# Scatters that add scaled expert rows to the image's rows, two-expert tiles spread, and one run of tiles for all four units

## The reference, cut to what matters

```python
x = x + conv0(ln_c(x))                   # gate from two line convolutions, softmax over channels
t = t + moe0(ln_t(t))                    # 8 experts, top 2, shares renormalised, tanh gelu
x = x + conv1(ln_c(x))                   # max pools of 7 sizes, two of them weighted by a score
t = t + moe1(ln_t(t))                    # 8 experts, top 2, shares not renormalised, gelu
# moe: logits = x @ Wr + br; p = softmax(logits); two largest; y = sum share_e * (gelu(x W1_e + b1_e) W2_e + b2_e)
```

## Time and profile before

| what | us |
|---|---|
| median of 3 runs (lowest to highest) | 983.96 (982.83 to 988.96) |
| the profiled run's own time | 989.66 |
| its span, first to last instruction | 986.8 |

### The profile page before, as it was taken

The page is one execution under the profiler, slowest core; times in us unless marked ns, Lnnn a source line. Parts: engine busy times, 40 slices in busy tenths (PEclk is TensorE's granted clock), DMA queues, the critical chain, the costliest instruction groups (busy, mean ns, idle before and its releaser), DMA issues.

```text
span 986.8 us, 14530 instructions
## 1 busy us (share of the span) xinstructions
PE 758.5 (77%) x4233; PEld 656.6 (67%) x4233; DVE 555.5 (56%) x1262; ACT 520.6 (53%) x1407; POOL 608.4 (62%) x597
## 2 busy tenths in 40 slices
PE   0766249999988798975789499976689977988760
PEld 0535238988887586864788387865679866776760
DVE  7967953263500198999867198999985004100005
ACT  1602427475565465653177376653287754555644
POOL 1000057777777777888632777888754777777760
PEclk9886569999999989999589699998699999999985
DMA  9000255455578483544136773543147856656537
GB/s 356 5 0 1 85 204 160 133 176 162 198 238 286 120 308 128 175 149 129 43 106 227 236 257 123 179 150 126 41 119 237 287 193 220 202 160 239 181 101 255
DMA packets 56861, 165.23 MB, mean 167 GB/s; under 512 B 13888, under 2 KB 13901, under 8 KB 56528
## 3 DMA queue, kind: packets, MB, share of 16 engines
q1 hardware_dynamic: 38608, 128.87, 38.5%
q0 software_dynamic: 18176, 35.44, 12.0%
HBM read 134.89 MB, written 31.20 MB: 168 GB/s over the span
## 4 chain that ended last, share of the span: by engine, by line
DVE 32%; PE 31%; POOL 16%; issue 8%; DMA 6%; ACT 5%; SPq 1%; POOLq 0%; DVEq 0%; ACTq 0%
PE h_ps L787 9%; POOL xg L515 8%; PE yT_ps L800 8%; POOL y_rows L524 8%; DVE state L1290 6%; DVE work L1276 5%; DVE work L1271 5%; DVE tok L1240 4%; PE acc_ps L739 4%; DMA xg<-xn_rows,tile_rows 3%; PE turn_ps L722 3%; PE acc_ps L759 3%; DVE work L1284 2%; DMA work<-y_rows 2%; DVE work L986 2%
## 5 line engine op out<-in xcount | busy, mean ns | idle before, releaser
L515 POOL DMA_INDIRECT xg<-xn_rows,tile_rows x284 | 301.5, 1062 | 226.7 <-DVEq L1206 123.8
L524 POOL DMA_INDIRECT y_rows<-yr,tile_rows x284 | 302.4, 1065 | 127.7 <-issue 82.3
L787 PE MATMUL h_ps<-xT,expert 128*128 128x256 f32 (+1 forms) x1376 | 295.3, 365 | 6.8 <-ACT hT L600 5.5
L600 ACT ACTIVATE hT<-h_ps,expert 128x256 f32<-128x256 f32 (+1 forms) x688 | 250.3, 442 | 72.0 <-PE h_ps L787 71.7
L800 PE MATMUL yT_ps<-hT,expert 128*128 128x256 f32 (+1 forms) x1376 | 278.8, 350 | 1.8 <-ACT yT L611 1.8
L787 PEld LDWEIGHTS h_ps<-xT,expert 128*128 128x128 f32 x1376 | 235.3, 205 | 29.3 <-issue 6.6
L800 PEld LDWEIGHTS yT_ps<-hT,expert 128*128 128x128 f32 x1376 | 233.7, 197 | 27.8 <-ACT yT L611 2.2
L1240 DVE SCALAR_TENSOR_TENSOR tok<-work,share,tok 128x128 f32<-128x128 f32 x224 | 62.3, 348 | 293.0 <-DMA work<-y_rows 292.3
L611 ACT ACTIVATE yT<-yT_ps,expert 128x256 f32<-128x256 f32 (+1 forms) x172 | 72.5, 440 | 116.7 <-PE yT_ps L800 116.6
L776 PE MATMUL xT_ps<-ident,xg 128*128 128x128 f32 x284 | 60.2, 294 | 88.4 <-DMA xg<-xn_rows,tile_rows 85.1
L588 ACT ACTIVATE xT<-xT_ps 128x256 f32<-128x256 f32 x144 | 55.6, 386 | 129.1 <-PE xT_ps L776 129.0
(11 more groups left out here) (202 smaller groups left out, 654.3 us busy)
## 6 DMA issues: line engine op xcount, KB each, us to landing
expert<-in_experts SPq DMA_DIRECT2D x172, 514.5 KB, 3.9
work<-y_rows SPq DMA_DIRECT2D x48, 256.0 KB, 6.2
xn_rows<-work SPq DMA_DIRECT2D x16, 512.0 KB, 6.3
xg<-xn_rows,tile_rows POOLq DMA_INDIRECT x284, 3.5
y_rows<-yr,tile_rows POOLq DMA_INDIRECT x284
tok<-in_x_tokens SPq DMA_DIRECT2D x8, 512.0 KB, 7.4
state<-in_x SPq DMA_DIRECT2D x2, 2048.0 KB, 17.4
work<-y_rows SPq DMA_DIRECT2D x8, 512.0 KB, 6.2
```

Of the source, the lines that this page charges most:

```text
L515: pool.indirect_dma_start(xg[:, s, h, :], None, xn_rows[unit], bass.IndirectOffsetOnAxis(ap=tile_rows[unit % 2][:, 0, at, h:h + 1], axis=0)) \
L524: pool.indirect_dma_start(y_rows[unit], bass.IndirectOffsetOnAxis(ap=tile_rows[unit % 2][:, 1, at, h:h + 1], axis=0), yr[:, s, h, :], None ...
L600: ins = act.activation(hT[:, s, c, cols], h_ps[c // 2][:, c % 2, cols], func, bias=expert[:, t.load(h) % W_RING, BIAS + c:BIAS + c + 1])
L787: mm = pe.matmul(h_ps[c // 2][:, c % 2, cols], expert[:, t.load(h) % W_RING, c * P:(c + 1) * P], xT[:, t.slot(2), cols], start=True, stop= ...
```

## The change

It has four parts, all in one edit.

1. **Scatters add.** `y_rows`, `load_outputs` of two rows, and `combine` are gone. Before a unit's first scatter, SP stores the image's rows to `sums` (`store_base`; for units 2 and 3 this is the output tensor itself). Each scatter adds its rows to the rows in DRAM (`compute_op=ALU.add`). A token can be in two tiles, so a tile's first scatter waits until the tile before has landed, and the second half of a two-expert tile waits for the first half. `load_outputs` then reads the sums of units 0 and 1 straight into the image's rows; the sums of units 2 and 3 are the output.
2. **Rows are scaled by slot.** The normalised rows in DRAM grow from 128 to 130 numbers: the share of the first choice, and the second share less the first. The gather brings them along. ScalarE makes the share of each seat from them and from `second`, which says whether the seat is a second choice (two 128x1 products in `copy_x`), and scales the copy to `yr` with it, one block at a time. VectorE works the shares out sooner (`shares`): from exponents of nine numbers, the ninth being the second largest logit.
3. **Two-expert tiles are spread** over the unit (`SPREAD`) instead of standing at its end; `SEAT` tells which blocks a tile takes. A two-expert tile's first half is scattered at the beginning of the step, ahead of the step's gathers, and the second half behind them.
4. **One run of all four units**; steps of `WHEN` for mixing move three tiles forward.

```diff
+SPREAD = [4, 8, 13, 17, 22, 26, 31, TILES - 1]
-RUNS = [(0, 1), (2, 3)]
+RUNS = [(0, 1, 2, 3)]
-    mixing(0, read=3, state=(6, 7, 8, 9), norm=11, route=(28, 28), slots=30.3, rows=(30, 31, 31.6, 33),
-           invert=(33, 33, 33, 33)),
-    mixing(1, read=2, state=(4, 5, 6, 7), norm=8, route=(25, 25), slots=27.3, rows=(27, 28, 28.6, 30),
-           invert=(30, 30, 30, 30)),
+    mixing(0, read=3, state=(5, 6, 7, 7.6), norm=8, route=(25, 25), slots=27.3, base=27, rows=(27, 28, 28.6, 30),
+           invert=(30, 30, 30, 30)),
+    mixing(1, read=2, state=(4, 4, 5, 5), norm=6, route=(22, 22), slots=24.3, base=24, rows=(24, 25, 25.6, 27),
+           invert=(27, 27, 27, 27)),
...
+            def store_base(u):
+                sp.wait_ge(s_stats, u + 2)
+                for q in range(QUARTERS):
+                    sp.dma_start(sums[u][:, quarter(q), :], tok[u % IMAGES][:, quarter(q), :]).then_inc(s_base[u], 16)
...
-                    pool.wait_ge(s_xt_ps, t.done(d - RING))
+                    pool.wait_ge(s_xt_sb, t.done(d - RING))
...
-            def scatter(t, d):
+            def scatter(t, d, *halves):
                 s = t.slot(RING, d)
                 unit, at = t.at(d)
-                pool.wait_ge(s_yr_sb, t.done(d))
-                for h in range(t.halves(d)):
-                    pool.indirect_dma_start(y_rows[unit],
...
+                for h in halves:
+                    if h == 0:
+                        pool.wait_ge(s_yr_sb, t.done(d))
+                        if at == 0:
+                            pool.wait_ge(s_base[unit], 16 * QUARTERS)
+                        else:
+                            pool.wait_ge(s_scat[t.slot(RING, d - 1)], t.landed(d - 1))
+                    elif t.parts(d) > 1:
+                        pool.wait_ge(s_scat[s], t.landed(d) - 16)
...
+                                            compute_op=ALU.add).then_inc(s_scat[s], 16)
...
                 def step(t, mid):
+                    due = range(t.halves(-S_BEHIND)) if t.has(-S_BEHIND) and t.at(-S_BEHIND)[1] < TILES - 1 else []
+                    early = 1 if due and t.parts(-S_BEHIND) > 1 else 0
+                    scatter(t, -S_BEHIND, *due[:early])
...
                         gather(t, G_AHEAD)
...
+                    scatter(t, -S_BEHIND, *due[early:])
...
+                for h in range(t.halves(d)):
+                    act.activation(share_of[:, r, h:h + 1], xg[:, r, h, P + 1:], ACT.Identity,
+                                   bias=xg[:, r, h, P:P + 1], scale=second[unit % 2][:, SEAT[at], h:h + 1])
...
-                act.activation(yr[:, s, :, :], yr_ps[:, 0:HALVES, :], ACT.Copy).then_inc(s_yr_sb, 1)
+                for h in range(t.halves(d)):
+                    ins = act.activation(yr[:, s, h, :], yr_ps[:, h, :], ACT.Copy, scale=share_of[:, s, h:h + 1])
...
-            for b in range(IMAGES):
-                combine(2 + b)
```

More of the change, by code:

```diff
@@ L45 @@
 EMPTY = 2 * PAIRS
+SHARES = 2
+SPREAD = [4, 8, 13, 17, 22, 26, 31, TILES - 1]
+SEAT = [FULL + SPREAD.index(j) if j in SPREAD else j - sum(i < j for i in SPREAD) for j in range(TILES)]
+FIRST_LOAD = [j + sum(i < j for i in SPREAD) for j in range(TILES)]
+TILE_OF_LOAD = [j for j in range(TILES) for _ in range(HALVES if j in SPREAD[:-1] else 1)]
 BIG = 3.0e38
@@ L69, with mixing @@
 AFTER_UP, AFTER_DOWN = 0.3, 0.6
-def mixing(b, read, state, norm, route, slots, rows, invert):
+def mixing(b, read, state, norm, route, slots, base, rows, invert):
     u = 2 + b
@@ L80, in mixing @@
     steps += [(slots, "route_slots", u), (slots, "route_exp", u)]
+    steps += [(base, "base_store", u)]
     steps += [(rows[q], "route_rows", u, q) for q in range(QUARTERS)]
@@ L150, in parts, with seat_runs @@
     def parts(self, d=0):
-        return self.halves(d) if self.at(d)[1] >= FULL else 1
+        return self.halves(d) if self.at(d)[1] in SPREAD else 1
     def load(self, h=0, d=0):
         unit, at = self.at(d)
-        return unit * LOADS + (at if at < FULL else FULL + HALVES * (at - FULL) + h)
+        return unit * LOADS + FIRST_LOAD[at] + h
+def seat_runs():
+    runs = []
+    for j in range(TILES):
+        single = j in SPREAD
+        size = (1 if j == TILES - 1 else HALVES) if single else 1
+        if not single and runs and runs[-1][3] == HALVES:
+            at, n, seat, step = runs[-1]
+            runs[-1] = (at, n + 1, seat, step)
+        else:
+            runs.append((FIRST_LOAD[j], size, HALVES * SEAT[j], 1 if single else HALVES))
+    return runs
+SEAT_RUNS = seat_runs()
 def columns(t, d=0):
@@ L299, in build @@
         tile_rows = [sb(f"tile_rows{i}", [P, 2, TILES, HALVES], U32) for i in range(2)]
+        second = [sb(f"second{i}", [P, TILES, HALVES]) for i in range(2)]
         gap_parts = sb("gap_parts", [P, GROUPS])
@@ L314, in build @@
         by_row = [m.rearrange("p (h w) -> p h w", h=SIDE)
-                  for m in (work[2][:], expert[:].rearrange("p w e -> p (w e)")[:, 0:TOKENS])]
+                  for m in (work[2], expert[:].rearrange("p w e -> p (w e)")[:, 0:TOKENS])]
         def one_hots(u, k):
@@ L371, in build @@
         s_scat = [sem(f"scattered{i}") for i in range(RING)]
[L372 to L375, removed]
+        s_share = sem("shares_ready")
+        s_base = [sem(f"sums{u}_begun") for u in range(UNITS)]
+        s_y_in = [[sem(f"sums{b}_piece{q}_loaded") for q in range(GROUPS)] for b in range(IMAGES)]
         PARAMETERS = 2
-        IDENT, CONSTS = 2, 25
+        IDENT, CONSTS = 2, 23 + len(SEAT_RUNS)
         BANKS = (1 + 2 * GROUPS + 3) + UNITS * (GROUPS + 2) + IMAGES * (2 * GROUPS + 2)
@@ L427, in store_normalised, with wait_scattered, load_outputs @@
                     sp.dma_start(xn_rows[u].rearrange("(p t) c -> p t c", t=BLOCKS)[:, quarter(q), :],
[L428 to L446, removed]
+                                 rows_out[:, quarter(q), :]).then_inc(s_xn_st[u], 16)
+            def wait_scattered(u):
+                last = Tile(u, TILES - 1)
+                for d in range(RING):
+                    sp.wait_ge(s_scat[last.slot(RING, -d)], last.landed(-d))
+            def load_outputs(b, *pieces):
+                wait_scattered(b)
+                for g in pieces:
+                    sp.dma_start(tok[b][:, group(g), :], sums[b][:, group(g), :]).then_inc(s_y_in[b][g], 16)
             def weights(u):
@@ L466, in _ @@
                 weights(u)
-            sp.wait_ge(s_done, 16 * sum(PIECES[u] for u in range(UNITS - IMAGES, UNITS)))
+            wait_scattered(UNITS - 1)
+            for u in range(UNITS - IMAGES, UNITS):
+                sp.wait_ge(s_base[u], 16 * QUARTERS)
         @block.gpsimd
```

164 lines of the change are left out of this document (73 added, 91 removed).

## The result

The changed kernel takes **1285.29 us** (median of four runs, 1283.58 to 1285.83) where the kernel before took 986.31 beside it: a ratio of 1.303, with a 95% interval of [1.298, 1.308]. The profiled run has a span of 1280.9 us, 294.1 more than before.

The account below looks back on a forecast made before the run. The prediction took GpSimd's queue of indirect DMAs as the bound: 902 us of span without landing waits plus 121 of waits gave 1023, or 1020 us of time (3.7% slower), with an 8-in-10 range of 945 to 1115.

Parts of the forecast that it names:

- I take no difference: GpSimd's issue of an adding scatter costs the same as a plain one; bounds from 9 us gained to 142 us added.
- Dear accumulation: Rival: scatter issue rises by a quarter or more, or landing passes 3.8 us; 1090 to 1200 us, chance 0.12 above 1115.
- The wait term, 121 us: GpSimd's scatters waiting for the tile before to land: 13 + 86 + 3 + 19 us over four kinds of places.
- L: Landing time of an adding scatter from its start, taken as 3.2 us; the forecast's case ran from 2.9 to 3.8.
- the tail's places: Seven places after the last gather, nothing between scatters of the last eight tiles: 7 x 2.7 = 19 us.
- an ordinary tile: L + 0.78 - 3.86: Wait before an ordinary tile's first scatter: landing plus restart less three issues as cover; 108 x 0.12 = 13 us.
- second halves: Two-expert tiles' second scatters, covered by two gathers as an ordinary tile is: 28 x 0.12 = 3 us.
- The 902 us without landing waits: Span of GpSimd's queue: 130 to first gather, 760 of issue, 9 of late-scatter waits, 3 of tail.
- of the 67 us I keep 9: GpSimd's waits for ScalarE and TensorE, with the seam between units 1 and 2, fall from 67 to 9 us.
- the seams don't close: Rival: first gathers of units 2 and 3 still wait for their rows; 10 to 20 us, 1030 to 1040, within the forecast's case.
- the saved tail: After the last scatter, output loads and the image's store go: about 3 of 24.1 us left, 21 saved.
- ScalarE's products: Two small products per tile and split scaling on ScalarE, at most 1.2 us a tile, hidden under GpSimd's 5.14: nothing.

Follow-up runs that it names:

- own rows, no wait: Changed kernel with adding scatters to rows of their own, so no scatter waits for the one before; half the result left out: 1116.46 us, 1.127.
- half rows: Kernel with adding scatters to rows of their own, each adding only 64 of a row's 128 numbers: 1112.74 us, 1.128.
- the 2 x 2: Four kernels: plain scatters to own rows without wait 979 us, with waits for landings 1087; adding scatters likewise 1116 and 1285 (the changed kernel).
- The kernel that is just this: Changed kernel with plain scatters to rows of their own and no wait for landings; half the result left out: 979.44 us, 0.989.
- one pooling size: Kernel with plain scatters to own rows and no wait (979.4 us), with one pooling size instead of all: 938.73 us, 0.951.
- the two parts put into it alone: Kernel before with rows scaled by slot, plain scatters and 16 sums for 64 products: 991.43 us, 1.004; kernel before in one run of tiles: 1009.16 us, 1.022.
- a shorter chain on VectorE: Kernel with plain scatters to own rows and no wait (979.4 us), with two pooling sizes fewer: 947.39 us; with one size only: 938.73 us.

## Why the prediction was wrong

Its direction and its pattern of waits were right, and the direction not by luck: with plain scatters the waits alone gave 1087 us. The time was 265 us short. Three terms, by its own steps:

1. **"I take no difference"** for the issue of an accumulating scatter. This is the step that failed most. It is 1.69 us where 1.065 was taken, 178 us in the changed kernel, beyond the upper end of 142. The rows compared two plain transfers with each other, and neither adds. The price is shown apart from waits and shared rows (own rows, no wait), and from bytes (half rows). "Dear accumulation" named it, at 1200 us at most, with a chance of 0.12 for all above 1115; it priced the issue with nothing of the seams beside it.
2. **The wait term, 121 us.** By the 2 x 2 it is 169 (108 with plain scatters). L was 3.2 in the sum and 3.7 in the trace, inside its case. Added up from the timeline, first halves waited 27 times for 83 us, 3.08 each (28 x 2.7 = 76 in the sum), and the tail's places some 20 (19). The part that failed is "an ordinary tile: L + 0.78 - 3.86": 13 us became 54, and second halves 3 became 19. The longer scatter even widened the cover, 1.99 + 2 x 1.285 = 4.56 against 3.7 + 0.78, so by the median no ordinary tile would wait at all; some 40 of 102 did, for 1.3 us each. Where they waited, the landing before them had taken 4.7 us in the median (31 places for which the trace has it), elsewhere 3.3 (30 places). Landings reach 8.0, and a wait is paid for each late one and not refunded by an early one.
3. **The 902 us without landing waits.** The kernel that is just this took 977.4 of span. Term by term: head 131.3 (130), issue 602.3 of busy time and 169.6 of gaps (597 and 163.5), tail 7.5 (3), and waits 66.7 where **"of the 67 us I keep 9"**. So 58 of the 75 us are waits that were to go, most of them at the seams. Moving the steps gave 12 us; with one pooling size, when the state can't be late, only 26 of the 66.7 go. The prediction read who releases GpSimd, and took GpSimd for the pace of the whole run. It also saw the joined run only as the end of a drain: the kernel before in one run shows that it sends unit 1's last scatters, and with them image 1's mixing, 21 us later. The chain of the page said VectorE 32%, TensorE 31%, GpSimd 16%; that line was there and was not weighed. The rival "the seams don't close" was right, but it was priced at 10 to 20 us. In the changed kernel itself the slow scatters hide these waits again (2.7 us for "ACT xT"), so this term and the first are not to be added in full. In times, by the prediction's own step from span to time, the 902 are 902 + 2.9 - 5.7 = 899 us where 979 was measured: 137 + 48 (169 - 121) + 80 = 265.

What held: the saved tail (17.4 of 21), ScalarE's products (6 us), no hole around 500 us, VectorE's 64 products gone for no gain. TensorE did not join the bound, though its granted clock fell from 0.884 to 0.825 over the span: it waits 297.9 us for gathered rows.

None of the runs points to a version that computes the whole result and beats the kernel before: the two parts put into it alone gave 1.004 and 1.022 (the second with steps of mixing of its own).

## What to carry to other kernels

Price a transfer that computes by itself before building on it: where the queue that issues it is near the bound, its issue time counts once for each transfer, and the nearest plain transfer is no bound. Cost a wait on a landing against the spread of landings, not the median, and put the wait two steps back if the data allow it: with rows of their own that wait cost nothing here, where waits one tile back cost 169 us. Before joining two runs of work on one queue, look at what then stands ahead of the last results of the first. And where the chain of waits names other engines than the waits of the busiest queue do, weigh the chain before pricing a seam: here a shorter chain on VectorE gave 32 to 41 us, and the joined run none.

## What the hardware showed unexpectedly

An indirect scatter of 128 rows that adds takes 1.69 us of GpSimd's time, a plain one 1.07, and 144 packets where a plain one takes 32; halving the rows' bytes changes neither. The landing of plain scatters, without shared rows and without waits (line L552 of that kernel), is

```profile
DMA to landing us min/median/max: 2.1/2.8/7.9
```

and the same line of the kernel with adding scatters:

```profile
DMA to landing us min/median/max: 2.7/4.3/8.5
```

The 0.6 us between the least values are no more than the longer issue (1.69 - 1.07); in the median it is 1.5, and 0.7 with half the bytes, which landed in 3.5. The Trainium skill ("DMA: Bandwidth & Descriptors", section "Anatomy of one DMA — SWDGE (gpsimd) path") has 2.0 us fixed and some more for the bytes, 2.15 as an estimate for 64 KB; only the quickest plain scatters come to that, and the median under load is 2.8.
